# Heads' attentions: the output product's units inside the step pattern, left-over projections between the first maxima, zeros issued by GpSimd

## The chip, the cores and the metric

The kernel runs on one core of a Trainium2 chip. A core has TensorE (PE: matmuls, with weight loads, PEld, beside them), VectorE (DVE), ScalarE (ACT), GpSimd (POOL) and SyncE (SP), which only issues DMAs; ACT and POOL issue DMAs too. The engines run their own instruction streams in order and wait for each other through semaphores. The metric is the device time in microseconds of one execution, median of several runs.

## The reference

Four layers over x (4 batches of 512 tokens, 256 wide) with a context of 1601 tokens. In each, a cross-attention and a feed-forward part are added to x through tanh gates. Layers 0, 1 and 2 have attentions of 16 heads of 16; layer 3 has one of a single head. Cut to what the change touches:

```python
for l in range(3):                                # attentions of heads
    q, k, v = norm(x) @ Wq + bq, ctx @ Wk + bk, ctx @ Wv + bv   # layer 1: rope on q and k; layers 1, 2: a mask
    attn = softmax(einsum("bhqd,bhkd->bhqk", q, k) * scale, axis=-1)
    x = x + tanh(g_xattn[l]) * (concat(einsum("bhqk,bhkd->bhqd", attn, v)) @ Wo + bo)
    x = x + tanh(g_ffn[l]) * ffn_l(norm(x))       # 0: a quantised linear, 1 and 2: 8 experts
x = x + tanh(g_xattn[3]) * one_head(norm(x), ctx)
x = x + tanh(g_ffn[3]) * top2_of_8_experts(norm(x))
```

## The kernel before, in words

Each heads' attention (`head_attention`) is written once as a list of units (`Plan`), and every engine's program walks that list and emits its share of each unit. So the order of the list is the order on every engine.

**Groups and steps.** The 16 heads of a batch are 4 groups of 4 heads; a layer has 4 batches x 4 groups = 16 groups, each in `attend`. A group walks the 1601 keys in 13 steps of 128. A step has four `s2` units (PE: scores of one head, 128 keys x 512 queries, L1348; ACT: exp of them, L1441) and ends with the `pv` unit of the step before (PE: four heads' exp times values, L1362).

**First pass.** The exp needs each query's maximum, which a first pass finds for a later group: 32 `max` units per group. One is, on PE, two matmuls of 401 keys (L1326, together an M) into one of two PSUM slots `m`, and on DVE one reduction of them (L1208). Which step holds how many M is a table: `FEW` or `MANY` gives the count for each of the 13 steps, `ORDER[count]` the pattern, with S for an `s2` unit and M for a `max` unit. After a group's 32nd M, `peak` (DVE, L1219 to L1223) and `turn` (PE transpose L1332, DVE copy L1228, then three small DMAs `qaug<-tm`) bring the maxima to where the group's first S needs them.

**Output product.** When two groups' attentions are normalised, `output` yields a `norm` unit (DVE multiplies 128x512, L1235) and two `out` units. One is two matmuls on PE (L1371) into an `m` slot and an addition into x on DVE (L1242). They are one of the `work` generators of `attend`: units handed out after an S by its number n, here `OUT_AT = 3, 6, 30` (3 units, from S 6 to S 30), on top of the step's M. `output` serves groups 1 and 3. Another such generator is `normalise`: `sum` (SP: `rc<-z`, `ot<-z`), `rec` (DVE reciprocal), `low` (ACT issues `sums<-rc`), `spread` (ACT waits for that DMA and issues `ot<-sums`).

**Start of layers 1 and 2** (`lay_out_ready`). Most keys and values were projected in the layer before; those of batch 3 are left (`LEFT`, class `Prepared`, `prepare_pe` and `prepare_act`): 8 key pieces and 13 value pieces in 4 chunks of the context (512, 512, 512 and 65 tokens), each chunk one DMA `e_t<-in_ctxT`. The list: queries of batch 0 (one half split in three bf16 parts by DVE, one by GpSimd, stored in DRAM as `qready`), their fetch for all groups into `qaug`, loads, `prep` k=0 (three chunks, 18 pieces), the 32 M of group 0, `turn`, `prep` k=1 (the last chunk, 3 pieces), the output bias, then the first group.

**Zeros.** In layer 2 the `take` units of batches 1 to 3 (ACT copies a group's values, L1435) also issue, on ACT's DMA queue, one of 12 transfers of 2 MB of zeros (`clear_act`: `xregion<-zero`, `yback<-zero`), for buffers of layer 3. ACT issues them after it has waited for the batch's values.

Of the kernel before, what the change touches and what calls it, by code (L numbers as in the profile page):

```python
# [170 lines left out]
class Prepared:  # L171
# [6 lines left out]
    def __init__(self, kn, sb, w, slots, order, in_parts, rope, plan):  # L178
# [17 lines left out]
        for count, engines in plan:  # L196
            part = []
            for _ in range(count):
# [18 lines left out]
                c["end"] = s  # L217
# [15 lines left out]
def prepare_weights_sp(kn, p):  # L233
# [4 lines left out]
    prepare_load_sp(kn, p, 3)  # L238
# [70 lines left out]
def prepare_pe(kn, p, part):  # L309
# [3 lines left out]
    for c in p.parts[part]:  # L313
        f, (c0, n) = c["i"] % 4, CHUNKS[c["n_c"]]
        arrived = kn.sema(f"p_ctx{f}", DMA)
        pe.wait_ge(arrived.sem, arrived.at(c["i"] // 4 + 1))
        for x in c["keys"]:
            j, s = x["j"], x["s"]
            if s >= many:
# [5 lines left out]
        for t, s in c["values"]:  # L325
            if s >= many:
                pe.wait_ge(p_free.sem, p_free.at(s - many + 1))
# [7 lines left out]
def prepare_act(kn, p, part):  # L335
# [4 lines left out]
    for c in p.parts[part]:  # L340
        c0, n = CHUNKS[c["n_c"]]
        for x in c["keys"]:
            j, s, k = x["j"], x["s"], x["k"]
            f, slot = k % p.RING, p.slots[s % many]
# [18 lines left out]
        if c["i"] >= 2:  # L363
            act.wait_ge(kept.sem, kept.at(c["i"] // 2))
        for i, (t, s) in enumerate(c["values"]):
            act.wait_ge(p_full.sem, p_full.at(s + 1))
            act.copy(p.vb[0:KW[t], f, i, :], p.slots[s % many][0:KW[t], 0:D]).then_inc(p_free.sem, 1)
        h, t0 = KW[t], c["values"][0][0]
# [100 lines left out]
class Plan:  # L469
# [91 lines left out]
    def attend(self, g, b, peaks, counts, *work):  # L561

        given = [0] * len(work)
        for k in range(KT):
            turning, j = bool(self.to_turn), 0
            for it in ORDER[counts[k]]:
                if it == "M":
                    next(peaks, None)
                    continue
# [17 lines left out]
    def lay_out(self):  # L587
# [36 lines left out]
        for b in range(B - 1):  # L624
# [4 lines left out]
            ended = [(self.output(1, b - 1), *OUT_AT)] if b else []  # L629
            self.attend(1, b, peaks, FEW, *ended, (projected, 16, 6, JOBS - 1), (self.normalise(0, b), NORM_STEPS, 2 * HG, NORM_LAST))  # L630
            self.attend(2, b, peaks, FEW, (projected, 10, 0, 20), (self.normalise(1, b), NORM_STEPS, 2 * HG, NORM_LAST))
            self.attend(3, b, peaks, FEW, (self.chain(self.then("fetch", b=b + 1, g=2, what="kq", k=1, by="kd2"),
                                                 *(self.then("take", b=b + 1, g=g) for g in range(3))), 4, 8, 24),
                        (self.output(0, b), *OUT_AT), (self.normalise(2, b), NORM_STEPS, 2 * HG, NORM_LAST))
# [12 lines left out]
    def lay_out_ready(self):  # L647
# [17 lines left out]
        for g in range(NG):  # L665
# [3 lines left out]
        for b in range(B):  # L669
# [7 lines left out]
            for g in range(1, NG):  # L677
                renew = [self.renew(g - 1, b + 1)] if on else []
                ended = [(self.output(0 if g == 3 else 1, b if g == 3 else b - 1), *OUT_AT)] if g == 3 or g == 1 and b else []
                self.attend(g, b, peaks, FEW if on or g < NG - 1 else (0,) * KT, *ended, *renew, *((k, *given) for k in keys), (self.normalise(g - 1, b), NORM_STEPS, 2 * HG, NORM_LAST))  # L680
# [24 lines left out]
def head_attention(kn, w, gate, scale, rope, mask, ready, setup, late):  # L705
# [4 lines left out]
    with ctx:  # L710
# [51 lines left out]
        if ready:  # L762
            room = dict(p_ctx=a.e_t[:].rearrange("p a j n -> p (a j n)").rearrange("p (f c n) -> p f c n", c=DC, n=512), p_kf=a.ot)
            if rope is not None:
# [3 lines left out]
                           [a.pv[:]] + [s[:] for s in a.s_slot], LEFT, (), None, ((3, ("",)), (1, ("",))))  # L768
# [208 lines left out]
def head_ready_sp(kn, a, n_of):  # L977
# [35 lines left out]
    for u in plan.units:  # L1013
# [12 lines left out]
        elif u.kind == "prep_loads":  # L1026
            prepare_weights_sp(kn, a.p)
            prepare_sp(kn, a.p, 0)
# [93 lines left out]
def head_pool(kn, a):  # L1122
# [122 lines left out]
def head_pe(kn, a):  # L1245
# [22 lines left out]
    for u in plan.units:  # L1268
# [26 lines left out]
        elif u.kind == "prep":  # L1295

            pe.wait_ge(s_free.sem, s_free.at(u.s))
            prepare_pe(kn, a.p, u.k)
            p_free = kn.sema("p_free")
            if u.k == 1:  # L1300
                pe.wait_ge(p_free.sem, p_free.at(a.p.n))
# [11 lines left out]
        elif u.kind == "max":  # L1313
            if (u.b, u.g) not in started:
# [5 lines left out]
                by, n = a.arrived[u.b, u.g, "k"]  # L1320
                pe.wait_ge(kn.sema(by, DMA).sem, kn.sema(by, DMA).at(n))
# [53 lines left out]
def head_act(kn, a):  # L1375
# [10 lines left out]
    for u in plan.units:  # L1386
# [28 lines left out]
        elif u.kind == "prep":  # L1415
            prepare_act(kn, a.p, u.k)
# [6 lines left out]
        elif u.kind == "take":  # L1423
# [6 lines left out]
            if a.clears and u.b:  # L1430
                clear_act(kn, a, (u.b - 1) * NG + u.g)
# [40 lines left out]
def clear_act(kn, a, nth):  # L1472

    act, cleared = kn.nc.scalar, kn.sema("cleared", DMA)
    parts = GATED_ROWS // REGION
    to, lo = (kn.dram["xregion"], REGION * nth) if nth < parts else (kn.dram["yback"], REGION * (nth - parts))
    if nth < CLEARED:
        width = to.shape[1]
        act.dma_start(to[lo:lo + REGION, :].rearrange("(p r) c -> p r c", p=P),
# [1660 lines left out]
```

## Time and profile before

| | us |
|---|---|
| median of 3 runs | 3765.19 (3760.28 to 3768.38) |
| the profiled execution | 3765.78 |
| its span in the profile | 3764.6 |
| PE busy | 3387.0 (90% of the span) |
| DVE busy | 2168.7 (58%) |
| ACT busy | 2024.8 (54%) |
| POOL busy | 943.5 (25%) |

The heads' attentions lie at 0 to 826 us (layer 0), 1006 to 1750 us (layer 1) and 2062 to 2806 us (layer 2) of the span. A number at a row's start is microseconds since the span's start; busy time says how long an engine had work, not that it was what the others waited for.

### The profile page before, as it was taken

How to read it: one execution, taken by the hardware profiler on the slowest of the kernel's cores; microseconds unless marked ns; L12 is line 12 of the kernel's file. 1: busy time of each engine (PE TensorE's matmuls, PEld its weight loads, DVE VectorE, ACT ScalarE, POOL GpSimd, SP SyncE). 2: the span in 40 equal slices, each digit the busy share in tenths (PEclk: the TensorE clock that was granted, in tenths of full speed). 3: DMA queues.
4: the chain of work that ended last, by engine and by line, in shares of the span. 5: the costliest groups of instructions: out<-in, count | busy, mean ns of one | idle time of the engine just before them, and what ended most of it. 6: DMA issues, size and time to landing. Idle time of an engine off the chain costs nothing.

```text
span 3764.6 us, 52382 instructions
## 1 busy us (share of the span) xinstructions
PE 3387.0 (90%) x18396; PEld 1786.1 (47%) x18396; DVE 2168.7 (58%) x3463; ACT 2024.8 (54%) x4490; POOL 943.5 (25%) x1061
## 2 busy tenths in 40 slices
PE   5999999978699999997898799999978979897997
PEld 2333333325432333333697323333327956697996
DVE  6667676837767787883302577878842033364333
ACT  2577767753236677775333266767752322254664
POOL 2232322004638462001302262410002010022332
PEclk8899999989789999998899799999998989998998
DMA  8142323115655453203764665654118421132555
GB/s 197 41 107 66 104 74 96 26 59 165 175 170 130 102 121 76 52 17 117 229 234 134 188 167 136 157 126 109 48 40 296 155 93 53 33 116 103 183 183 170
DMA packets 265310, 456.02 MB, mean 121 GB/s; under 512 B 54027, under 2 KB 174643, under 8 KB 262875
## 3 DMA queue, kind: packets, MB, share of 16 engines
q1 hardware_dynamic: 163878, 224.05, 22.3%
q0 software_dynamic: 49520, 166.30, 13.4%
q10 hardware_dynamic: 51653, 62.32, 5.8%
q8 instruction: 150, 2.46, 0.3%
q14 instruction: 109, 0.89, 0.1%
HBM read 292.46 MB, written 153.91 MB: 119 GB/s over the span
## 4 chain that ended last, share of the span: by engine, by line
PE 76%; DVE 8%; DMA 6%; ACT 3%; POOL 3%; issue 2%; SPq 1%; ACTq 0%; POOLq 0%; DVEq 0%
PE pv L1362 15%; PE s L1348 14%; PE m L1326 13%; PE h L2849 5%; PE y L2857 5%; PE h L2423 4%; PE y L2432 4%; DVE mxp L1208 3%; PE y L1829 3%; PE s L1809 2%; PE s L1293 2%; PE m L1371 2%; DMA sums<-rc 1%; PE s L1310 1%; ACT e_t L1441 1%
## 5 line engine op out<-in xcount | busy, mean ns | idle before, releaser
L1208 DVE TENSOR_REDUCE mxp<-m 128x1 f32<-128x802 f32 x1536 | 1445.1, 987 | 487.4 <-PE m L1326 485.2
L1441 ACT ACTIVATE e_t<-s 128x512 f32<-128x512 f32 (+1 forms) x2496 | 1330.0, 600 | 514.7 <-PE s L1348 492.0
L1348 PE MATMUL s<-qaug,kaug 100*128 100x512 bf16 (+1 forms) x2496 | 834.6, 386 | 34.5 <-ACT e_t L1441 28.0
L1326 PE MATMUL m<-kaug,qaug 97*128 97x401 bf16 x3072 | 811.2, 347 | 34.6 <-DVE mxp L1208 16.8
L1362 PE MATMUL pv<-e_t,v 128*32 128x512 f32 (+1 forms) x4992 | 671.6, 610 | 0.2
L1326 PEld LDWEIGHTS m<-kaug,qaug 97*128 97x128 bf16 x3072 | 258.9, 99 | 551.2 <-DVE mxp L1208 303.7
L1348 PEld LDWEIGHTS s<-qaug,kaug 100*128 100x128 bf16 (+1 forms) x2496 | 244.6, 100 | 579.3 <-ACT e_t L1441 390.3
L127 POOL TENSOR_TENSOR rstd<-rstd,mhalf 128x16 f32<-128x16 f32 (+2 forms) x9 | 24.3, 2697 | 1105.5 <-DVE rstd L120 1105.5
L2919 ACT ACTIVATE ez<-h,b 128x128 f32<-128x128 f32 x440 | 120.1, 388 | 160.4 <-PE h L2849 160.4
L1362 PEld LDWEIGHTS pv<-e_t,v 128*32 128x32 f32 (+1 forms) x4992 | 98.7, 108 | 215.1 <-ACT e_t L1441 156.2
L2310 DVE SCALAR_TENSOR_TENSOR y<-y,b 128x256 f32<-128x256 f32 x39 | 16.6, 425 | 302.3 <-PE y L2432 302.3
L2721 DVE TENSOR_SCALAR ez<-ez 128x1024 f32<-128x1024 f32 x55 | 38.2, 694 | 225.6 <-ACT z L2919 225.6
L1085 POOL TENSOR_TENSOR kr<-kf,ks 128x512 f32<-128x512 f32 (+1 forms) x78 | 78.8, 1011 | 343.0 <-ACT ks L1413 339.1
L2506 ACT ACTIVATE hT<-h,b 128x128 f32<-128x128 f32 x312 | 84.9, 383 | 128.3 <-PE h L2423 128.2
L2423 PE MATMUL h<-xtT,w 128*128 128x128 f32 x1248 | 149.2, 279 | 0.4 <-ACT xtT L2523 0.3
L2857 PE MATMUL y<-w,hT 128*128 x624 | 143.0, 383 | 5.8 <-DVE hT L2722 5.8
L2849 PE MATMUL h<-xtT,w 128*128 128x128 f32 x1248 | 147.8, 277 | 0.0
L2423 PEld LDWEIGHTS h<-xtT,w 128*128 128x128 f32 x1248 | 146.0, 196 | 1.1 <-ACT xtT L2523 1.0
L2849 PEld LDWEIGHTS h<-xtT,w 128*128 128x128 f32 x1248 | 144.7, 194 | 0.1
L2432 PE MATMUL y<-w,hT 128*128 x624 | 140.9, 379 | 0.0
L2857 PEld LDWEIGHTS y<-w,hT 128*128 128x128 f32 x624 | 116.7, 192 | 21.0 <-issue 6.4
L2919 ACT ACTIVATE z<-h,b 128x128 f32<-128x128 f32 x440 | 122.8, 453 | 0.0
(384 smaller groups left out, 3834.0 us busy)
## 6 DMA issues: line engine op xcount, KB each, us to landing
w<-in_L_w POOLq DMA_DIRECT2D x78, 1024.0 KB, 5.3
w<-in_L_w SPq DMA_DIRECT2D x24, 1024.0 KB, 12.5
xregion<-zero ACTq DMA_DIRECT2D x10, 2056.0 KB, 12.4
kaug<-kparts SPq DMA_DIRECT2D x16, 1200.8 KB
kaug<-kready SPq DMA_DIRECT2D x32, 600.4 KB
kaug<-kready SPq DMA_DIRECT2D x16, 1200.8 KB
vn<-values SPq DMA_DIRECT2D x8, 1536.0 KB
values<-p_vb ACTq DMA_DIRECT2D x21, 512.0 KB, 5.3
```

The costliest lines, as they stand in the source:

```text
L1208: dve.tensor_reduce(a.mxp[:, u.g % 2, half, n:n + 1], a.m_slot[u.m % 2][:].rearrange("p (a n) -> p a n", a=2)[:, :, 0:PIECE + 1], AX.XY, A ...
L1326: m = pe.matmul(slot[:, 512 * k:512 * k + PIECE + 1], a.qaug[0:R_MAX, u.g, j, P * qc:P * qc + P], a.kaug[0:R_MAX, u.g, j, k0:k0 + PIECE + ...
L1348: pe.matmul(slot[0:KW[u.k], :], a.kaug[0:R_ALL, u.g, u.j, P * u.k:P * u.k + KW[u.k]], a.qaug[0:R_ALL, u.g, u.j, :], start=True, stop=True) ...
L1362: m = pe.matmul(a.pv[32 * j:32 * j + 32, :], a.v[0:KW[u.k], u.k, u.g, VW * j:VW * j + 32], a.e_t[0:KW[u.k], u.n % 2, j, :], start=u.k == 0 ...
L1441: act.activation(a.e_t[0:KW[u.k], e % 2, u.j, :], a.s_slot[u.s % 3][0:KW[u.k], :], ACT.Exp).then_inc(s_free.sem, 1)
L1829: m = pe.matmul(a.y_slot[:, 0:D], a.eT[0:KW[i], k % 2, i, :], a.v[0:KW[i], b % 2, i, :], start=i == 0, stop=i == KT - 1)
L2423: m = pe.matmul(a.h_slot[i % 2][:, P * f:P * f + P], a.w1[:, w1_at, c, P * f:P * f + P], xT(c), start=c == 0, stop=c == DC - 1)
L2432: m = pe.matmul(a.y_slot[i % 2][:, 0:D], a.hT[:, i % 2, f, :], w2(f), start=f == 0, stop=f == FC - 1)
L2506: t = act.activation(a.hT[:, p, f, :], slot[:, P * f:P * f + P], func, bias=bias(f))
L2849: m = pe.matmul(a.h_slot[i % 2][:, P * f:P * f + P], w1[:, c, P * f:P * f + P], xT(c), start=c == 0, stop=c == DC - 1)
L2857: m = pe.matmul(a.y_slot[i % 2][:, 0:D], a.hT[:, i % 2, f, :], w2(f), start=f == 0, stop=f == FC - 1)
L2919: t = act.activation(to[:, p, P * f:P * f + P], slot[:, P * f:P * f + P], func, bias=bias(f))
```

## The change

Four edits.

1. **Output units in the pattern.** In groups with an output product, `output` is no longer a `work` generator. Steps 3 and 6 use `OUT_ORDER = "MSSOSSM"`: the pattern for three M with O, one `out` unit, in place of the middle M. The counts of such groups are `FEW_OUT`, also 32 M. `norm` now has no place of its own: it stands right before the first `out`. Five groups of layer 0 and six each of layers 1 and 2 are changed, 17 in all; the last batch of layer 0 and the last group of layers 1 and 2 keep the old way.
2. **First maxima.** The first group of a layer has five M in its first step, two of them ahead of the first S (`"MMSMSSMS"`), where there were four.
3. **Left-over projections between the first maxima** (layers 1 and 2). Six pieces stand ahead, the other 15 one after every second M. Both halves of the first queries are split by DVE; group 0's queries are stored and fetched first; only one context chunk is loaded ahead of that, the other three behind it.
4. **Zeros on GpSimd.** The 12 transfers are issued by GpSimd, in its order of units, without the wait for the values.

```diff
-MANY = (4, 4, 3, 4, 3, 4, 3, 4, 3, 1, 1, 2, 2)
-ORDER = ("SSSS", "SMSSS", "SMSMSS", "MSSMSSM", "MSMSMSSM")
+MANY = (5, 4, 3, 4, 3, 4, 3, 4, 3, 1, 1, 2, 2)
+ORDER = ("SSSS", "SMSSS", "SMSMSS", "MSSMSSM", "MSMSMSSM", "MMSMSSMS")
...
+OUT_STEPS = (3, 6)
+OUT_ORDER = "MSSOSSM"
+FEW_OUT = (3, 3, 3, 2, 3, 3, 2, 3, 2, 2, 1, 2, 3)
+LEFT_PIECES = KT + DC * len(CHUNKS)
+LEFT_AHEAD = 6
...
     def output(self, c, b):
         self.add("norm", b=b, g=2 * c + 1)
-        yield
         for k in range(TT // 2):
...
-            for it in ORDER[counts[k]]:
+            for it in ORDER[counts[k]] if out is None or k not in OUT_STEPS else OUT_ORDER:
...
+                if it == "O":
+                    next(out)
+                    continue
...
         for c in range(DC):
-            self.split("q", 0, c, 0, ("dve", "pool"))
-        self.add("fetch", b=0, g=0, what="q", k=NG, by="qd")
+            self.split("q", 0, c, 0, ("dve",))
+            if c == 0:
+                self.add("fetch", b=0, g=0, what="q", k=1, by="qd")
+                self.add("prep_more")
+            else:
+                self.add("fetch", b=0, g=1, what="q", k=NG - 1, by="qd")
+        self.add("fetch", b=0, g=1, what="k", k=1, by="kd1")
         self.add("loads", b=0)
-        for g in range(1, NG):
+        for g in range(2, NG):
             self.add("fetch", b=0, g=g, what="k", k=1, by=f"kd{g}")
-        self.add("prep", k=0)
-        for _ in self.maxima(0, 0):
-            pass
+        pieces = iter(range(LEFT_PIECES))
+        for _ in range(LEFT_AHEAD):
+            self.add("prep", k=next(pieces))
+        for n, _ in enumerate(self.maxima(0, 0)):
+            if n % 2:
+                k = next(pieces, None)
+                if k is not None:
+                    self.add("prep", k=k)
         self.turn()
-        self.add("prep", k=1)
+        for k in pieces:
+            self.add("prep", k=k)
         self.add("bias")
+        self.add("prep_end")
...
+        elif u.kind == "take" and a.clears and u.b:
+            pool.wait_ge(filled.sem, filled.at(2))
+            clear_pool(kn, a, (u.b - 1) * NG + u.g)
...
-            if a.clears and u.b:
-                clear_act(kn, a, (u.b - 1) * NG + u.g)
```

**PE at the start of layer 1.** L322 and L330 (L327 and L337 after) are a left-over key and value piece, L1326 (L1376) an M. Before:

```order
L330 MATMUL s_107<-p_wv,e_t 128x256 x2
L322 MATMUL s_108<-e_t,p_wk 128x512 x2
L322 MATMUL s_109<-e_t,p_wk 128x512 x2
L330 MATMUL pv<-p_wv,e_t 128x256 x2
L330 MATMUL s_107<-p_wv,e_t 128x256 x2
L330 MATMUL s_108<-p_wv,e_t 128x256 x2
```

After, from the same piece on:

```order
L337 MATMUL s_107<-p_wv,e_t 128x256 x2
L1376 MATMUL m_110<-kaug,qaug 128x401 x2
L1376 MATMUL m_111<-kaug,qaug 128x401 x2
L327 MATMUL s_108<-e_t,p_wk 128x512 x2
L1376 MATMUL m_110<-kaug,qaug 128x401 x2
L1376 MATMUL m_111<-kaug,qaug 128x401 x2
L327 MATMUL s_109<-e_t,p_wk 128x512 x2
```

The first M stood behind 18 pieces and now stands behind 6; the others lie between pairs of M.

**SP at the same place**, with its waits: L252 loads a context chunk, L94 stores queries, L1050 (L1088) fetches them. Before:

```order
L252 DMA e_t_99<-in_ctxT 128x2x512 x3
L252 DMA e_t_99<-in_ctxT 128x2x65
L94 DMA qready<-ks_94 128x3x512 [waits split_dve]
L94 DMA qready<-ks_94 128x2x512
L94 DMA qready<-ks_94 128x512
L1050 DMA qaug_96<-qready 96x16x512 [waits pooled1,stored0]
```

After:

```order
L252 DMA e_t_99<-in_ctxT 128x2x512
L94 DMA qready<-ks_94 128x3x512 [waits split_dve]
L94 DMA qready<-ks_94 128x2x512
L94 DMA qready<-ks_94 128x512
L1088 DMA qaug_96<-qready 96x4x512 [waits stored0]
L252 DMA e_t_99<-in_ctxT 128x2x512 x2
L252 DMA e_t_99<-in_ctxT 128x2x65
```

The fetch of group 0's queries no longer waits for GpSimd's half, and three chunks moved behind it.

**DVE around the first output unit of a group** (layer 1). L1208 (L1255) reduces an M, L1235 (L1282) is `norm`, L1242 (L1289) the output unit's addition. Before:

```order
L1235 TENSOR_TENSOR ot<-ot 128x512 [waits summed,moved]
L1208 TENSOR_REDUCE mxp<-m_110 128x1 [waits m_full]
L1208 TENSOR_REDUCE mxp<-m_111 128x1 [waits m_full]
L1208 TENSOR_REDUCE mxp<-m_110 128x1 [waits m_full]
L1208 TENSOR_REDUCE mxp<-m_111 128x1 [waits m_full]
L1208 TENSOR_REDUCE mxp<-m_110 128x1 [waits m_full]
L1242 SCALAR_TENSOR_TENSOR x<-m_111,gates,x 128x512 [waits m_full]
```

After:

```order
L1255 TENSOR_REDUCE mxp<-m_111 128x1 [waits m_full]
L1255 TENSOR_REDUCE mxp<-m_110 128x1 [waits m_full]
L1282 TENSOR_TENSOR ot<-ot 128x512 [waits summed,moved]
L1289 SCALAR_TENSOR_TENSOR x<-m_111,gates,x 128x512 [waits m_full]
L1278 RECIPROCAL rc<-rc 128x16 [waits summed]
```

`norm` moved from five reductions ahead of the addition to right before it, behind the reduction of the step's first M.

## Rows read from the trace of the kernel before

**Rows 1.** The page, part 4: the chain that ended last, by engine.

```profile
PE 76%; DVE 8%; DMA 6%; ACT 3%; POOL 3%; issue 2%; SPq 1%; ACTq 0%; POOLq 0%; DVEq 0%
```

**Rows 2.** Timeline, layer 1's start: start us, us, engine line op, [idle before <-releaser].

```profile
1036.95 3.60 PE L322 MATMUL s<-e_t,p_wk 128*128 128x512 f32 x8
...
1050.73 0.85 PE L1326 MATMUL m<-kaug,qaug 97*128 97x401 bf16 x4
...
1051.27 30.71 DVE L1208 TENSOR_REDUCE mxp<-m 128x1 f32<-128x802 f32 x32 [23.54 <-PE m L1326]
...
1090.18 0.63 PE L1348 MATMUL s<-qaug,kaug 100*128 100x512 bf16 x1
```

**Rows 3.** Timeline, layer 2's start.

```profile
2091.43 3.60 PE L322 MATMUL s<-e_t,p_wk 128*128 128x512 f32 x8
...
2105.20 0.85 PE L1326 MATMUL m<-kaug,qaug 97*128 97x401 bf16 x4
...
2144.65 0.63 PE L1348 MATMUL s<-qaug,kaug 100*128 100x512 bf16 x1
```

**Rows 4.** Timeline, layer 0's start, value pieces between its M.

```profile
76.34 26.00 DVE L1208 TENSOR_REDUCE mxp<-m 128x1 f32<-128x802 f32 x28 [0.72 <-PE m L1326]
...
106.47 0.88 PE L1326 MATMUL m<-kaug,qaug 97*128 97x401 bf16 x2
108.14 0.61 PE L1348 MATMUL s<-qaug,kaug 100*128 100x512 bf16 x1 [0.80 <-DMA qaug<-tm]
```

**Rows 5.** Timeline, SP's issues at layer 1's start.

```profile
1027.76 1.69 SPq L94 DMA_DIRECT2D qready<-ks  x3
1039.05 0.33 SPq L1050 DMA_DIRECT2D qaug<-qready  x1
```

**Rows 6.** Windows, layer 1's start: stretch, us, busy by engine, PEclk, DMA share, GB/s.

```profile
1065.00:1070.00 5.00, 4.34 (x12) 0.65 (x10) 4.91 (x6) 0.00 (x0) 0.00 (x0) 0.50 1.03 209
1075.00:1080.00 5.00, 4.35 (x11) 0.65 (x10) 4.90 (x6) 0.00 (x0) 0.00 (x0) 0.50 0.00 1
```

**Rows 7.** Timeline, layer 1, batch 2, group 3: step 3 and the next.

```profile
1563.08 1.06 PE L1362 MATMUL pv<-e_t,v 128*32 128x512 f32 x8
...
1564.31 0.51 PE L1326 MATMUL m<-kaug,qaug 97*128 97x401 bf16 x2
...
1564.85 1.89 DVE L1208 TENSOR_REDUCE mxp<-m 128x1 f32<-128x802 f32 x2 [0.51 <-PE m L1326]
...
1565.90 1.13 PE L1371 MATMUL m<-wo,ot 128*128 128x256 f32 x4 [0.31 <-DVE mxp L1208]
1566.87 0.38 PE L1348 MATMUL s<-qaug,kaug 100*128 100x512 bf16 x1
...
1567.18 1.07 PE L1362 MATMUL pv<-e_t,v 128*32 128x512 f32 x8
...
1570.27 1.06 PE L1362 MATMUL pv<-e_t,v 128*32 128x512 f32 x8
```

**Rows 8.** DVE groups by form, 1400 to 1750 us: count, busy us, mean ns.

```profile
L1235 DVE TENSOR_TENSOR ot<-ot 128x512 f32<-128x512 f32 x4 | 2.7, 682 | 0.0
```

**Rows 9.** Windows, whole groups: layer 2 (first three), layer 1 (last three).

```profile
2196.34:2241.07 44.73, 40.47 (x223) 12.53 (x222) 31.57 (x40) 28.83 (x56) 28.05 (x39) 0.92 0.73 182
2318.98:2368.42 49.44, 43.41 (x230) 13.94 (x229) 31.64 (x40) 29.98 (x58) 39.95 (x45) 0.93 0.72 200
2487.34:2537.86 50.52, 43.91 (x231) 14.12 (x230) 31.64 (x40) 30.03 (x58) 15.03 (x16) 0.90 0.53 143
1147.52:1190.10 42.58, 39.45 (x222) 12.20 (x222) 32.02 (x40) 28.80 (x56) 39.42 (x44) 0.96 0.67 158
1482.08:1522.47 40.39, 39.78 (x231) 13.54 (x230) 33.14 (x43) 28.88 (x56) 0.00 (x0) 1.00 0.25 49
1522.47:1560.00 37.53, 37.53 (x223) 12.22 (x222) 31.07 (x40) 28.66 (x56) 0.00 (x0) 1.00 0.28 53
```

**Rows 10.** Chain of waits, layer 2: start us, us, what.

```profile
2333.40 18.65 DMA sums<-rc
```

More of the change, by code:

```diff
@@ L216, in __init__ @@
                     s += 1
-                c["end"] = s
+                c["end"], c["many"] = s, len(c["keys"]) + len(c["values"])
                 self.chunks.append(c)
@@ L306, in prepare_held_sp, with prepare_pe @@
         prepare_store_sp(kn, p, x)
-def prepare_pe(kn, p, part):
+def prepare_pe(kn, p, part, only=None):
     pe, p_full, p_free, p_w = kn.nc.tensor, kn.sema("p_full"), kn.sema("p_free"), kn.sema("p_w", DMA)
@@ L313, in prepare_pe @@
     for c in p.parts[part]:
+        if only is not None and not c["end"] - c["many"] <= only < c["end"]:
+            continue
         f, (c0, n) = c["i"] % 4, CHUNKS[c["n_c"]]
@@ L318, in prepare_pe @@
             j, s = x["j"], x["s"]
+            if only not in (None, s):
+                continue
             if s >= many:
@@ L325, in prepare_pe @@
         for t, s in c["values"]:
+            if only not in (None, s):
+                continue
             if s >= many:
@@ L332, in prepare_pe, with prepare_act @@
             m.then_inc(p_full.sem, 1)
-def prepare_act(kn, p, part):
+def prepare_act(kn, p, part, only=None):
     act, p_full, p_free, p_w = kn.nc.scalar, kn.sema("p_full"), kn.sema("p_free"), kn.sema("p_w", DMA)
@@ L341, in prepare_act @@
         c0, n = CHUNKS[c["n_c"]]
+        if only is not None and not c["end"] - c["many"] <= only < c["end"]:
+            continue
         for x in c["keys"]:
             j, s, k = x["j"], x["s"], x["k"]
+            if only not in (None, s):
+                continue
             f, slot = k % p.RING, p.slots[s % many]
@@ L362, in prepare_act @@
         kept = kn.sema(f"p_v{f}", DMA)
-        if c["i"] >= 2:
+        if c["i"] >= 2 and only in (None, c["values"][0][1]):
             act.wait_ge(kept.sem, kept.at(c["i"] // 2))
         for i, (t, s) in enumerate(c["values"]):
+            if only not in (None, s):
+                continue
             act.wait_ge(p_full.sem, p_full.at(s + 1))
             act.copy(p.vb[0:KW[t], f, i, :], p.slots[s % many][0:KW[t], 0:D]).then_inc(p_free.sem, 1)
+        if only not in (None, s):
+            continue
         h, t0 = KW[t], c["values"][0][0]
@@ L559, in output, with attend @@
             yield
-    def attend(self, g, b, peaks, counts, *work):
+    def attend(self, g, b, peaks, counts, *work, out=None):
         given = [0] * len(work)
@@ L679, in lay_out_ready @@
                 ended = [(self.output(0 if g == 3 else 1, b if g == 3 else b - 1), *OUT_AT)] if g == 3 or g == 1 and b else []
-                self.attend(g, b, peaks, FEW if on or g < NG - 1 else (0,) * KT, *ended, *renew, *((k, *given) for k in keys), (self.normalise(g - 1, b), NORM_STEPS, 2 * HG, NORM_LAST))
+                last_one = not on and g == NG - 1
+                self.attend(g, b, peaks, (0,) * KT if last_one else FEW_OUT if ended else FEW, *(ended if last_one else []), *renew, *((k, *given) for k in keys), (self.normalise(g - 1, b), NORM_STEPS, 2 * HG, NORM_LAST),
+                            out=ended[0][0] if ended and not last_one else None)
             last = (self.renew(NG - 1, b + 1), (self.normalise(NG - 1, b), NORM_STEPS, 2 * HG, NORM_LAST))
@@ L1026, in head_ready_sp @@
         elif u.kind == "prep_loads":
-            prepare_weights_sp(kn, a.p)
-            prepare_sp(kn, a.p, 0)
+            prepare_weights_sp(kn, a.p, 1)
+        elif u.kind == "prep_more":
+            prepare_load_sp(kn, a.p, len(a.p.chunks))
         elif u.kind == "loads":
@@ L1143, in head_pool @@
         elif u.kind in ("q", "k") and u.by == "pool":
+            i = splits.index(u)
+            for x in splits[i + 1:][0:1] if a.ready else ():
+                if x.kind == "k" and splits[i - 1].by == "dve":
+                    by_dve = kn.sema("split_dve")
+                    pool.wait_ge(by_dve.sem, by_dve.at(splits[i - 1].n + 1))
+                    head_load_pool(kn, a, x)
             head_split(kn, a, u, pool, "pool")
@@ L1319, in head_pe @@
                     pe.wait_ge(kn.sema(by, DMA).sem, kn.sema(by, DMA).at(n))
-                by, n = a.arrived[u.b, u.g, "k"]
-                pe.wait_ge(kn.sema(by, DMA).sem, kn.sema(by, DMA).at(n))
+                for it in ("q", "k"):
+                    if (u.b, u.g, it) in a.arrived:
+                        by, n = a.arrived[u.b, u.g, it]
+                        pe.wait_ge(kn.sema(by, DMA).sem, kn.sema(by, DMA).at(n))
             j, qc, half = u.k // (2 * QC), u.k // 2 % QC, u.k % 2
@@ L1415, in head_act @@
         elif u.kind == "prep":
[L1416 removed]
+            prepare_act(kn, a.p, 0, u.k)
         elif u.kind == "v":
```

30 lines of the change are left out of this document (16 added, 14 removed).

## The prediction

> **What bounds the kernel now.** I read the page's chain first: PE carries 76% of it [rows 1], so the kernel is as long as PE's program plus the time in which PE waits or runs slowly. Then windows over whole groups of the attentions show two kinds. In an undisturbed group of layer 1 PE is busy for the whole 37.53 us at full clock, or 39.78 of 40.39 us where output units are in it; in three groups of layer 2 it idles 4.3, 6.0 and 6.6 us at a mean clock of 0.90 to 0.93 [rows 9]. In the steady part only PE's own instructions and their order count. The rest lies in the disturbed groups, and at the starts of layers 1 and 2, which the timeline shows: PE first works off pieces of left-over projections, then feeds the 32 first M, and there DVE is the bound, with 32 reductions back to back in 30.71 us while PE is fed at half clock [rows 2, 6].
>
> **Left-over projections between the M.** Before, PE comes to its seventh piece at 1036.95 and to the first M at 1050.73; after, the M follow the sixth piece. That is 13.78 us earlier, if queries and keys are there. In layer 2 it is 2105.20 - 2091.43 = 13.77 us [rows 2, 3].
> The M then take longer only where a piece makes PE slower than DVE. Layer 0 has this very pattern, with value pieces, and its 28 reductions took 26.00 us, 0.93 each [rows 4], a little less than the 0.96 before (30.71 / 32). A key piece takes 1.8 us of PE (3.60 for two [rows 2]), to which two M of some 0.35 us come (802 columns each at full clock, 2.4 GHz, are 0.33): 2.5 us per pair against 1.86 on DVE. Four large key pieces lie there, so 4 x 0.65 = 2.6 us. From first M to last reduction: 32 x 0.93 + 0.5 + 2.6 = 32.9 us, against 1051.27 + 30.71 - 1050.73 = 31.25. That costs 1.6 us.
> Behind the last reduction, layer 1 needed 1090.18 - 1081.98 = 8.20 us to its first S, with three pieces in the way. In layer 0, with none, it was 108.14 - 102.34 = 5.80 us [rows 4]. That gives 2.4 us. Sum per layer: 13.8 - 1.6 + 2.4 = 14.6 us. What can be late next are DMAs. The fetch of the first queries was issued at 1039.05, after GpSimd's half had been stored; now it waits for DVE's first half alone, whose store was issued at 1027.76 [rows 5] and will be earlier, so it can land before 1037. The three context chunks now follow it. The DMA engines were full until shortly before 1075 (share 1.03, then 0.00 [rows 6]) and the small transfers of the maxima, which now come near 1071, stand in SP's queue behind that load. I take off 0.6 us in each layer: 14 us, two layers, **28 us less**. The bounds are 2 x 7 (queries or chunks 7 us late) and 2 x 16.
>
> **One more early M.** While PE waits for the maxima to be moved (0.80 us at 108.14), it now has a second M. At the half clock of that place an M takes 0.88 us [rows 4]. Three layers, 0 to 2.6 us; I take **2 us less**.
>
> **Output units.** Step 3 took 1567.18 - 1563.08 = 4.10 us, and a step with three M takes 1570.27 - 1567.18 = 3.09 us [rows 7]. Over whole groups an output unit cost (40.39 - 37.53) / 2 = 1.43 us [rows 9], though PE is held by it for only 1566.87 - 1565.90 = 0.97. It stood as a third user of two slots, 0.31 us of it waiting for a reduction. In the place of the middle M it needs no slot that isn't free: 3.09 - 0.35 + 0.97 = 3.7 us, 0.4 less than 4.10. The counts with three, two and one M are the same in both tables, so nothing else changes.
> But the first unit of a group now has `norm` right ahead of it in DVE's order, and PE waits for it. After the step's first M starts, DVE takes 0.54 us to begin its reduction (1564.31 to 1564.85), 0.95 for it (1.89 for two) and 0.68 for `norm` [rows 7, 8]; PE follows 0.1 us later, as at 1565.90. That is 2.27 us, where PE would come to the unit after one M and two S, 0.35 + 2 x 0.22 = 0.79 us (an S is 512 columns, 0.21). So PE, with everything behind it, stands 1.5 us: 3.7 + 1.5 = 5.2 us instead of 4.1. Before, `norm` lay five reductions earlier and nothing waited for it. Per group +1.1 - 0.4 = +0.7 us, in 17 groups **12 us more**. Below, without any stall: 17 x (-0.8) = -14. Above, with DVE one reduction (0.95) further behind: +28. I take the middle, since each of its pieces has a row.
>
> **Zeros on GpSimd.** In layer 2 `sums<-rc`, 8 KB, landed 18.65 us after issue, and so in the chain [rows 10]; in ACT's program the batch's zeros, 2 MB, are issued shortly ahead of it on the same queue. ACT waits for it in `spread`, ahead of exps that PE needs. The three disturbed groups lost 44.73 - 37.53 = 7.2 us, and, allowing 3.6 us for two query projections at 1.8, 49.44 - 41.1 = 8.3 and 50.52 - 41.1 = 9.4: 25 us in all [rows 9]. The like group of layer 1, with no zeros at all, lost 42.58 - 37.53 = 5.05 us, so that much of the first remains. That leaves 20 us. Not all of it comes back: GpSimd waits for nothing of ACT, so it sends the zeros of a batch in a row as soon as its splits are done, and five of them (10 MB) right behind its last split, near 2500 us, when the batch's values are loaded too. I take **15 us less**; bounds 0 and 25. What stays hidden: 12 issues gone from ACT, which has idle time in each step, and come to GpSimd, behind whose last ones nothing waits for 300 us.
> Here a page speaks against the change. The Trainium skill (DMA: Bandwidth & Descriptors, Issuing engines are not separate DMA queues) says that all DMAs run on the same 16 engines whoever issues them, and that another issuer saves only the sequencer's time. Another section of it (Queues, rings and completion order) says that a DMA engine goes round its queues packet by packet, by which a small transfer passes a large one of another queue. No row of before decides between them; the first is a rival below.
>
> **Sum.** Against the profiled execution's own 3765.8 us (span 3764.6, and 1.2 around it; the median is 0.6 lower): -28 - 2 + 12 - 15 = -33, so 3733 us.
>
> **Rivals.**
> *The zeros only change their issuer.* Same DMA engines, same bytes, so `sums<-rc` lands as late and only the issue time on ACT is saved, which ACT has to spare. For it: the DMA share was 0.53 to 0.73 over those groups, and the group without zeros still lost 5 us. Against: in that group it was at 0.67, and it lost less than the two later ones. Time: 3733 + 15 = 3748. By the page's first rule this is what happens.
> *The output units run without a stall,* if DVE is ahead when the step begins, or `norm` overlaps the S. For it: DVE is busy only 31.07 of 37.53 us. Against: the reduction of the step's own M is in front of `norm`, and starts 0.54 us after it whatever DVE's slack. Time: 3733 - 17 x 1.5 = 3708 with all of it, 3714 if a part stays.
> *The DMA engines become the bound at the starts.* The load up to 1075 is the same, and the maxima's small transfers cannot pass it in SP's queue. If it also slips by the gap in which SP waits for the first store (up to 7 us), half of the gain goes: 3733 + 14 = 3747.
> *Slower: the run of zeros is served in order of arrival.* Place: layer 2, batch 2 to 3, five transfers of 2 MB in a row. At the 143 to 200 GB/s of those stretches [rows 9] each takes 10 us or more; a small transfer behind all five is 50 us late, of which the steps between `low` and `spread` hide about 10. PE then stands 40 us: 3748 + 40 = 3788. It decides from two queued ahead on. Against: no row of before shows a transfer of one queue held up for the whole of another queue's.
> *The change doesn't do what it says:* the order shows pieces, units and issues moved as described, so this is left with no chance.
>
> **Numbers.** Chances: forecast 0.50, zeros without gain 0.17, no stall 0.13, bound by DMA at the starts 0.12, slower 0.05, and 0.03 for gains that cancel to nothing. Range: 3714 to 3752 holds the first four and what lies between. 0.2% is 7.5 us and about what a measurement of this kernel can tell from no change. Faster by more: 0.90; within: 0.05; slower: 0.05.
>
> **What would show it.** In layers 1 and 2 the first M starts 14 us earlier against the first piece, reductions run at 0.93 us with four gaps near 0.6, and the first S comes 5.8 us behind the last. In step 3 of the 17 groups the `out` matmul waits about 1.5 us for the `norm` line of DVE, in step 6 for nothing; groups take 41.1 us, not 40.4. In layer 2 `sums<-rc` lands in under 10 us and the three groups come to some 43, 42 and 44 us. I am wrong if the first M waits for a DMA, if step 3 shows no wait, or if the three groups keep their length.

## The result, and the profile after

The changed kernel takes 3774.7 us (median of 8 runs, 3769.8 to 3778.1), the kernel before 3767.5 beside it; the ratio is 1.0019, with a 95% interval of 1.0010 to 1.0028. So it is 0.2% slower, where 3733 us were forecast. The profiled execution has a span of 3773.7 us against 3764.6.

The page's chain by engine, after (answers to [rows 1]), and its line of the chain by instruction:

```profile
PE 74%; DMA 8%; DVE 8%; ACT 3%; issue 2%; POOL 2%; SPq 2%; ACTq 0%; POOLq 0%; DVEq 0%
PE pv L1412 15%; PE s L1398 14%; PE m L1376 13%; PE h L2897 5%; PE y L2905 5%; PE h L2471 4%; PE y L2480 4%; DVE mxp L1255 3%; PE y L1877 2%; PE s L1857 2%; PE s L1340 2%; DMA rc<-z 2%; PE m L1421 1%; DMA qaug<-tm 1%; PE s L1358 1%
```

PE's share fell by two points and that of the DMAs rose by two. The names are new too: before, the one DMA that the chain's line named was `sums<-rc`; now it names `rc<-z` and `qaug<-tm`, transfers of 8 KB and 4 KB.

To find where that is, I followed the start of each group's first `pv` from layer to layer. From the first `pv` of a layer to its last, layer 0 takes 700.6 us (before: 700.0), layer 1 644.0 (644.5), layer 2 684.9 (645.6). The first `pv` of layer 1 comes 14.6 us earlier than before, that of layer 2 28.4. So everything up to 2123 us is a gain, about as forecast, and layer 2's attentions give back 39 us. These are readings of one execution each, and they scatter: in e2 and e7 below, whose programs are that of the kernel before up to layer 2, the first `pv` of layer 1 comes at 1088.7 and 1088.9 us instead of 1096.9. The windows over whole groups show it (columns as in [rows 9], to which they answer: the first, third and fifth are the three groups of layer 2 shown there, the second, fourth and sixth the groups behind them, the last two are in layer 1):

```profile
2167.18:2212.39 45.21, 40.57 (x222) 12.38 (x221) 32.21 (x41) 29.24 (x56) 32.93 (x44) 0.94 0.92 214
2212.39:2262.09 49.70, 43.12 (x224) 13.11 (x223) 31.20 (x40) 29.04 (x55) 0.00 (x0) 0.85 0.39 103
2302.33:2354.99 52.66, 45.69 (x232) 14.69 (x232) 32.80 (x41) 31.18 (x59) 39.43 (x44) 0.89 0.72 204
2354.99:2409.80 54.81, 44.00 (x229) 14.23 (x228) 33.99 (x42) 28.58 (x54) 30.40 (x41) 0.84 0.89 200
2488.86:2538.79 49.93, 45.67 (x232) 14.68 (x232) 32.66 (x41) 31.18 (x59) 20.79 (x21) 0.89 0.81 197
2538.79:2588.64 49.85, 43.16 (x228) 14.27 (x228) 32.60 (x41) 28.18 (x54) 0.00 (x0) 0.91 0.49 157
1466.75:1506.99 40.24, 38.90 (x228) 13.47 (x227) 32.59 (x42) 28.62 (x55) 0.00 (x0) 1.00 0.23 46
1506.99:1544.95 37.96, 37.96 (x225) 12.38 (x224) 31.74 (x41) 29.04 (x56) 0.00 (x0) 1.00 0.30 55
```

The three groups with long waits were 44.73, 49.44 and 50.52 us before: two are longer now, and the third is 0.6 us shorter. The three behind them, nearly undisturbed before, are now 10 to 15 us longer than their like of layer 1. In the groups in which PE has these long waits its mean granted clock is lower as well, 0.84 in the longest, so such a stall costs more than its own length.

The chain of layer 2 names the DMAs on it (start us, us, what; the pieces of PE and DVE between them left out):

```profile
2166.26 9.46 DMA rc<-z
...
2179.34 11.74 DMA sums<-rc
...
2198.56 6.83 DMA qaug<-tm
...
2209.98 17.03 DMA rc<-z
...
2334.06 12.03 DMA qaug<-tm
...
2387.99 13.58 DMA qaug<-tm
...
2520.45 9.44 DMA qaug<-tm
...
2535.71 18.61 DMA rc<-z
```

And the timeline shows what was issued just ahead of one of them (rows of GpSimd, SyncE and PE, about 2332 us):

```profile
2332.27 1.17 POOL L1527 DMA_DIRECT2D xregion<-zero  x1
...
2332.86 2.70 SPq L1115 DMA_DIRECT2D qaug<-tm  x3
...
2346.14 1.03 PE L1398 MATMUL s<-qaug,kaug 100*128 100x512 bf16 x2 [6.78 <-DMA qaug<-tm]
```

GpSimd issues 2 MB of zeros 0.6 us before SyncE issues the 4 KB of `qaug<-tm`. Such a transfer lands in 1.7 us (median) in layer 1, where there are no zeros; the last of these three took 12.0, and PE stands 6.8 us in front of its S.

What the small transfers do behind the run of five near 2510 us is of weight for the causes below. These are the DMA issues of two windows, 2509.4 to 2515 us and 2519.1 to 2521.1 us (size of one, median us from issue to landing):

```profile
xregion<-zero POOLq DMA_DIRECT2D x3, 2056.0 KB, 24.5
yback<-zero POOLq DMA_DIRECT2D x2, 2048.0 KB, 42.8
...
qaug<-tm SPq DMA_DIRECT2D x3, 4.0 KB, 9.1
```

The three of 4 KB were issued after all five of 2 MB and had landed by 2529.9 us. Of the five only the first had landed then; the others followed between 2535 and 2559 us. So the small ones were held up by some 7 us, but did not wait for all that was queued ahead of them.

Layer 1's start, after (answers to [rows 2]):

```profile
1025.62 3.75 PE L327 MATMUL pv<-e_t,p_wk 128*128 128x512 f32 x4 [8.02 <-DMA e_t<-in_ctxT]
...
1034.41 0.85 PE L1376 MATMUL m<-kaug,qaug 97*128 97x401 bf16 x4
...
1066.72 1.89 DVE L1255 TENSOR_REDUCE mxp<-m 128x1 f32<-128x802 f32 x2 [1.38 <-PE m L1376]
...
1075.83 0.61 PE L1398 MATMUL s<-qaug,kaug 100*128 100x512 bf16 x1 [1.53 <-DMA qaug<-tm]
```

Step 3 of the group in layer 1, batch 2, group 3, after (answers to [rows 7]):

```profile
1549.59 0.99 DVE L1255 TENSOR_REDUCE mxp<-m 128x1 f32<-128x802 f32 x1 [0.29 <-PE m L1376]
1550.50 0.68 DVE L1282 TENSOR_TENSOR ot<-ot 128x512 f32<-128x512 f32 x1
1551.33 1.10 PE L1421 MATMUL m<-wo,ot 128*128 128x256 f32 x4 [1.34 <-DVE ot L1282]
...
1553.13 1.06 PE L1412 MATMUL pv<-e_t,v 128*32 128x512 f32 x8
```

The output unit waits 1.34 us for `norm`, which stands behind the reduction of the step's own M, as forecast.

### The profile page after: what moved, and what is told of

The parts are those of the page before. It is cut to its first block, busy times and chain, and to the rows that moved or that the text cites. A ratio compares the mean times of both kernels' runs of the same rounds, so it can differ in the third digit from the quotient of the medians.

```text
span 3773.7 us, 52460 instructions
## 1 busy us (share of the span) xinstructions
PE 3363.4 (89%) x18396; PEld 1791.2 (47%) x18396; DVE 2176.6 (58%) x3476; ACT 2028.8 (54%) x4490; POOL 938.3 (25%) x1054
## 4 chain that ended last, share of the span: by engine, by line
PE 74%; DMA 8%; DVE 8%; ACT 3%; issue 2%; POOL 2%; SPq 2%; ACTq 0%; POOLq 0%; DVEq 0%
PE pv L1412 15%; PE s L1398 14%; PE m L1376 13%; PE h L2897 5%; PE y L2905 5%; PE h L2471 4%; PE y L2480 4%; DVE mxp L1255 3%; PE y L1877 2%; PE s L1857 2%; PE s L1340 2%; DMA rc<-z 2%; PE m L1421 1%; DMA qaug<-tm 1%; PE s L1358 1%
## 5 line engine op out<-in xcount | busy, mean ns | idle before, releaser
L1255 DVE TENSOR_REDUCE mxp<-m 128x1 f32<-128x802 f32 x1536 | 1448.7, 987 | 470.9 <-PE m L1376 468.8
L1376 PE MATMUL m<-kaug,qaug 97*128 97x401 bf16 x3072 | 801.2, 344 | 42.2 <-DVE mxp L1255 24.1
L1376 PEld LDWEIGHTS m<-kaug,qaug 97*128 97x128 bf16 x3072 | 259.6, 99 | 576.2 <-DVE mxp L1255 308.4
L2905 PEld LDWEIGHTS y<-w,hT 128*128 128x128 f32 x624 | 117.1, 193 | 20.7 <-issue 6.5
L2480 PEld LDWEIGHTS y<-w,hT 128*128 128x128 f32 x624 | 116.1, 191 | 14.0
## 6 DMA issues: line engine op xcount, KB each, us to landing
xregion<-zero POOLq DMA_DIRECT2D x10, 2056.0 KB, 15.5
```

The source lines that it names most:

```text
L1255: dve.tensor_reduce(a.mxp[:, u.g % 2, half, n:n + 1], a.m_slot[u.m % 2][:].rearrange("p (a n) -> p a n", a=2)[:, :, 0:PIECE + 1], AX.XY, A ...
L1376: m = pe.matmul(slot[:, 512 * k:512 * k + PIECE + 1], a.qaug[0:R_MAX, u.g, j, P * qc:P * qc + P], a.kaug[0:R_MAX, u.g, j, k0:k0 + PIECE + ...
L2480: m = pe.matmul(a.y_slot[i % 2][:, 0:D], a.hT[:, i % 2, f, :], w2(f), start=f == 0, stop=f == FC - 1)
L2905: m = pe.matmul(a.y_slot[i % 2][:, 0:D], a.hT[:, i % 2, f, :], w2(f), start=f == 0, stop=f == FC - 1)
```

## The experiments

**What theories there were.** From the two profiles: A, the zeros' transfers cost what layer 2 lost, because GpSimd issues them at moments at which a small transfer of the maxima or sums comes next, and that one lands late. B, something else of the change (start, units, early M) disturbs layer 2. Within A: A1, only the moment counts; A2, transfers that GpSimd issues are worse wherever they stand.

**e1 (the label's first part names each run): the zeros back on ScalarE, at `take`; all else as changed.**

```diff
-        elif u.kind == "take" and a.clears and u.b:
-            pool.wait_ge(filled.sem, filled.at(2))
-            clear_pool(kn, a, (u.b - 1) * NG + u.g)
...
+            if a.clears and u.b:
+                clear_act(kn, a, (u.b - 1) * NG + u.g)
```

> The changed kernel, but the 12 transfers of zeros are issued by ACT at the `take` units, as in the kernel before. Layer 2's attentions took 684.9 us from first to last pv in the changed kernel and 645.6 in the one before, so if the zeros' new issuer and moment are the whole loss (theory A), the time falls by 39 us, to 3736 us (3730 to 3742), and the two starts keep their 28 us. Rival B, that the output units or the earlier start of layer 2 brought the loss: the time stays above 3760 us.

Measured: 3741.0 us (3737.7 to 3744.1), ratio to before 0.9941 (0.9924 to 0.9957). Layer 2's attentions take 649.7 us, not 684.9. That is A, for 35 of the 39 us; the other edits disturb layer 2 by at most 4 us (645.6 before). The three longest DMAs of its chain are the kind that the kernel before had, `sums<-rc`:

```profile
2178.67 14.36 DMA sums<-rc
...
2304.48 19.32 DMA sums<-rc
...
2477.63 17.42 DMA sums<-rc
```

**e2: the kernel before, with this one edit of the change (zeros issued by GpSimd).**

> The kernel before, with only the zeros moved to GpSimd. Theory A: layer 2's attentions get some 39 us longer, 3800 to 3808 us. Rival B: within 8 us of the kernel before, since then the loss needs the other edits.

Measured: 3792.1 us (3790.0 to 3797.4), ratio 1.0081 (1.0064 to 1.0098): 28.7 us slower than before, in layer 2 (673.3 us against 645.6). The edit costs time by itself. The size is less than the 37 us or more that I had expected. That the zeros fall at another place against the groups in each kernel is my explanation; it was not tested.

**e3: the changed kernel, GpSimd's zeros held back to a fixed step of the group.** In front of each transfer GpSimd waits for the batch's values and for the fourth `pv` behind the group whose values are replaced, so that it falls beside `sums<-rc`.

```diff
             pool.wait_ge(filled.sem, filled.at(2))
+            pool.wait_ge(vl.sem, vl.at(2 * u.b + 2))
+            pool.wait_ge(pv_done.sem, pv_done.at(read.n + 5))
             clear_pool(kn, a, (u.b - 1) * NG + u.g)
```

> The changed kernel, but GpSimd waits before each transfer of zeros until the batch's values are there and the next group's fourth pv is done, so that each is issued within some 2 us of where ACT issued it (after the reciprocal, well ahead of the maxima's small transfers). Theory A1, it is the moment: zeros in flight hold every small transfer, and GpSimd issued them right ahead of those of the maxima (12 us instead of 1.7) and of `rc<-z`; then this run has neither these nor the `sums<-rc` behind zeros on ACT's queue: 3718 to 3732 us. Rival A2, it is the software queue that crowds out the others: the loss stays, 3760 us or more.

Measured: 3722.1 us (3720.0 to 3724.7), ratio 0.9891 (0.9874 to 0.9907). The same issuer, the same bytes, and some 50 us less than the changed kernel. That rules out A2 and shows A1. Ten of the twelve transfers are issued within 0.5 us of `sums<-rc`. Of the other two one came 6.2 us behind it and one 15.5, and just at the latter the chain has its longest DMA:

```profile
2312.02 1.17 POOL L1532 DMA_DIRECT2D xregion<-zero  x1
...
2312.60 2.69 SPq L1115 DMA_DIRECT2D qaug<-tm  x3
...
2325.79 1.03 PE L1403 MATMUL s<-qaug,kaug 100*128 100x512 bf16 x2 [6.69 <-DMA qaug<-tm]
```

**e4: the zeros on ScalarE, but right behind `sums<-rc` instead of ahead of it.**

```diff
             head_low_act(kn, a, u)
+            if a.clears:
+                clear_act(kn, a, u.n)
```

> The changed kernel, with the zeros on ACT's queue, but right behind `sums<-rc` (the `low` unit) instead of at `take`, in the first 12 groups. By A1 the zeros are done before the next maxima's transfers and nothing needed stands behind them on ACT's queue but `ot<-sums`: 3715 to 3728 us, 8 to 20 less than e1. By A2 the same. A third theory, A3, that any 2 MB anywhere in a group costs a stall of 5 us or so in the groups with other traffic: 3735 us or more.

Measured: 3714.2 us (3711.3 to 3717.7), ratio 0.9867 (0.9850 to 0.9883), 1 us below the forecast's range and 27 less than e1; A3 is out. Layer 2's attentions take 625.7 us, 20 less than before the change and 24 less than e1's. The timeline about 2300 us shows the place that the zeros have now: the next small transfer comes 15.7 us behind them, and by the page's row one transfer of zeros lands after 12.3 us (median).

```profile
2300.09 0.33 ACTq L1508 DMA_DIRECT2D sums<-rc  x1
...
2300.45 0.70 ACTq L1526 DMA_DIRECT2D xregion<-zero  x1
...
2316.15 1.79 SPq L1115 DMA_DIRECT2D qaug<-tm  x3
```

The page of e4, part 6, and below it the issues of 2300.4 to 2302 us and of 2316 to 2318.2 us: size of one and median us to its landing.

```profile
xregion<-zero ACTq DMA_DIRECT2D x10, 2056.0 KB, 12.3
...
xregion<-zero ACTq DMA_DIRECT2D x1, 2056.0 KB, 23.7
...
qaug<-tm SPq DMA_DIRECT2D x3, 4.0 KB, 7.0
```

Just at this place, where the next batch's values are loaded too (`vn<-values`, issued 1 to 2 us ahead), the gap is not enough: the zeros need 23.7 us, `qaug<-tm` takes 7.0, and PE stands 2.8 us. In the other groups the gap holds.

**e7: the kernel before, with the zeros at that place and nothing else changed.** Its edit is that of e4.

> The kernel before with one edit: ScalarE issues the 2 MB of zeros right behind `sums<-rc` of each head instead of at `take`. Theory M (the moment alone decides): the stalls of the layer-2 groups that the zeros cause go, as they do with the other edits in place; 3763 - 24 = 3739 us (3735 to 3746), where 24 is -49 for all edits with the zeros there, less -28 for the starts, -2 for the early M and +5 for the units. Rival I (it needs the earlier start, which moves the zeros away from other loads): within 8 us of 3763.

Measured: 3739.7 us (3729.3 to 3745.4), ratio 0.9939 (0.9922 to 0.9956). In layer 2's attentions the moment is worth 24 us without the rest of the change (645.6 to 622.0) and with it (649.7 to 625.7, e1 to e4); rival I is out. The three disturbed groups of [rows 9] take 37.6, 42.7 and 41.1 us here: that is about what they are when the zeros stand in nobody's way.

**e9: the changed kernel, each transfer of zeros cut into four.** What it asks is whether a small transfer waits for the one big transfer in hand or for all the bytes ahead of it.

```diff
-        pool.dma_start(to[lo:lo + REGION, :].rearrange("(p r) c -> p r c", p=P),
+        for r0, r1 in zip(cuts, cuts[1:]):
+            pool.dma_start(to[lo:lo + REGION, :].rearrange("(p r) c -> p r c", p=P)[:, r0:r1, :],
```

> The changed kernel with each 2 MB transfer of zeros by GpSimd split into four of a quarter of the rows, issued one behind the other at the same place. What is asked is how a 4 KB transfer on SyncE's queue comes to take 9 to 14 us behind one of 2 MB on GpSimd's. Theory Q (it is served behind all bytes already queued, whichever way they are cut): `qaug<-tm` of layer 2's groups still lands in 9 to 14 us, and the time stays within 8 us of 3775. Theory D (it waits only for the one transfer in hand): it lands in under 5 us, most of the 35 to 39 us of layer 2 comes back, 3738 to 3750 us. The 36 extra issues cost GpSimd about 1.2 us each, spread over 300 us, with nothing waiting behind them for long.

Measured: 3777.7 us (3768.0 to 3783.2), ratio 1.0018 (1.0008 to 1.0028): as slow as uncut. The chain has the same long landings (start us, us, what). So theory D is out, and to cut the transfers in four does not help. The numbers that theory Q gave came in, but its mechanism, that a small transfer is served behind all bytes already queued, does not hold either: in the run of 20 quarters (issued 2514.5 to 2529.4 us) `qaug<-tm` came behind 14 of them and landed in 9.5 us (median; 10.4 in the chain), while only 6 of the 14 had landed by then. What sets the 9 to 12 us stays open.

```profile
2213.75 22.03 DMA rc<-z
...
2341.38 11.59 DMA qaug<-tm
...
2402.29 18.70 DMA rc<-z
```

**e10: the kernel before, with the part on the starts alone.** Units, early M and zeros are as before.

> The kernel before with one part of the change alone: the pieces of the left-over projections between the M of the starts, with the early fetch of the first queries; units, early M and zeros as before. The forecast's term: 28 us less (14 in each of layers 1 and 2), 3763 - 28 = 3735 us (3731 to 3739), the first step of layer 1's attentions 14 to 15 us earlier, that of layer 2 28. Rival: the earlier start runs into the zeros and loads of layer 2 and gives a part back there: 3742 to 3752 us.

Measured: 3742.4 us (3738.7 to 3745.3), beside 3768.8 for the kernel before; ratio 0.9933 (0.9920 to 0.9946), 26 us less; 28 were forecast. The time itself lies at the lower end of the rival's 3742 to 3752, because the kernel before took 6 us more beside it than the 3763 from which both theories started; by the ratio it would be 3738, inside the forecast's range. In the trace the first `pv` of layer 2 comes 29.4 us earlier, and layer 2's attentions take 650.1 us against 645.6, nearly all of it in one group (53.8 us against 49.4, with a `sums<-rc` of 20.1 us where it was 18.7): the rival's effect is there, at 4 us in one execution.

**e6: e4, with the output units put back to their old place.**

> The kernel with the zeros issued by ScalarE right behind `sums<-rc` (3714 us), with the output units put back where they were in the kernel before: third users of the two slots, beside all M of their step, `norm` five reductions ahead. Theory by the traces (the pair of groups 78.2 against 77.9 us): the new place costs 0.28 us a group, so this is 17 x 0.28 = 5 us faster, 3709 us. Theory of the forecast (0.7 us a group): 12 us faster, 3702 us. Rival: the new place is a gain outside layer 1's even groups: slower than 3714.

Measured: 3712.7 us (3701.6 to 3715.6), ratio 0.9858 (0.9838 to 0.9878), against 0.9867 for e4: 3 us less by the ratios, which their intervals tell neither from nothing nor from 12. The traces decide for the 5 us: layers 0 and 1 are 2.3 and 2.5 us shorter than in e4, layer 2 as long. In the pair of groups the new place costs 40.24 + 37.96 = 78.20 us against 40.39 + 37.53 = 77.92 [rows 9].

**e5: e4, with `norm` five reductions ahead of its output unit again, the units in their new place.**

```diff
         self.add("norm", b=b, g=2 * c + 1)
+        yield
...
+                if out is not None and n == 6:
+                    next(out)
```

> The kernel with the zeros issued by ScalarE right behind `sums<-rc` (3714 us), and `norm` moved from right ahead of its output unit in step 3 to S number 6 of the group, five reductions earlier, as it was in the kernel before; the units keep their place in the pattern. Theory N: step 3 takes 5.1 us because the unit waits for `norm`, which stands behind the reduction of the step's own M; with `norm` done before, the step falls to 3.6 us like step 6, in 17 groups: 17 x 1.5 = 25 us less, 3689 us (3684 to 3698). Rival: the unit waits for its slot or for the next reduction, whatever `norm` does; step 3 keeps over 4.5 us and the time stays within 6 us of 3714.

Measured: 3690.5 us (3687.7 to 3701.0), ratio 0.9812 (0.9795 to 0.9830), at the forecast of theory N. In the trace the unit no longer waits, the step is 3.5 us instead of 5.1, and the group 38.84 us, all of it PE's. The timeline of that step, and the window of its group (columns as in [rows 9]):

```profile
1537.42 1.06 PE L1412 MATMUL pv<-e_t,v 128*32 128x512 f32 x8
...
1539.21 1.03 PE L1421 MATMUL m<-wo,ot 128*128 128x256 f32 x4
...
1540.94 1.06 PE L1412 MATMUL pv<-e_t,v 128*32 128x512 f32 x8
```

```profile
1534.15:1572.99 38.84, 38.84 (x228) 13.40 (x227) 32.49 (x42) 28.65 (x55) 0.00 (x0) 1.00 0.24 47
```

This kernel is the fastest of all here, 1.9% below the kernel before and 2.1% below the changed one by the ratios.

**e8: e4, without the early M.**

> The kernel with the zeros issued by ScalarE right behind `sums<-rc` (3714 us), with four M instead of five in the first step of each layer's first group. Forecast's theory: the fifth M fills a wait of PE, so it is worth 2 us and this takes 3716 us (3714 to 3718). Rival from the traces (layer 0's first step 4.7 us with it, 3.1 without): the fifth M only lengthens the step, and this takes 3710 to 3713 us.

Measured: 3720.8 us (3718.3 to 3723.2), ratio 0.9887 (0.9870 to 0.9904) against 0.9867. So the rival (the M only lengthens the step) finds no support: all runs of e8 lie above all of e4. The ratios are 7 us apart, but each has an interval of 0.0017 either way, so that the forecast's 2 us are as possible. The fifth M stands ahead of the first `pv`, so the place to look is the stretch from the last of the first 32 reductions to that `pv`: 13.2 us against 12.3 in layer 0, 11.5 against 12.3 in layer 2, and in layer 1 it scatters from 13.0 to 17.8 us among kernels with the same edits there. From the first `pv` on, the traces show 1 us either way (layer 0: 701.8 us against 700.7; layer 2: 624.6 against 625.7). So its size, and by the traces even its sign, stays open.

## Why the prediction was wrong

**The step that failed is the zeros: "I take 15 us less; bounds 0 and 25".** By e1 against the changed kernel it is 29 us more by the ratios (1.0019 - 0.9941), and 35 in layer 2's steps. This term's error, some 44 us, is more than that of the whole (42); the other terms were off by 7 us the other way (units) and 2 this way (starts).

The wait that I priced did go. In the kernel before, two steps of 9.7 and 10.6 us (in the groups from 2318.98 and 2487.34) waited for `sums<-rc`; after, both are 3.1 us, and ScalarE comes to its next issue behind `sums<-rc` 9.0 us after it (2316.76 to 2325.73), where it was 18.7. What I had at nothing are the new waits, and they cost more than the old ones.

Three things in that step were wrong.
- *I looked for the one small transfer that the zeros had delayed and not for those that they could delay.* A group has three in its critical order: `qaug<-tm` for the maxima, some 10 us later `rc<-z`, 12 to 15 us after that `sums<-rc`, and 16 us on the next `qaug<-tm` (e4's timeline). ScalarE issued the zeros 3 us ahead of `sums<-rc`, for which ScalarE waits only in `spread`, with about 9 us of cover (cover: the time from a transfer's issue until someone needs it). Moved to GpSimd, they met `qaug<-tm`, in front of which PE has 5 us of cover (in the chain from 2334.1, waited for from 2346.1 - 6.8 = 2339.4), and `rc<-z`, which took 17.0 and 18.6 us. There DVE stands, 7.2 us in the first case (2219.8 to 2227.0), with the reductions behind it.
- *I priced the order of GpSimd's program but not the clock time at which it issues.* GpSimd waits for nothing of ScalarE, as the prediction says; that was read as harmless. It means that nothing keeps the zeros away from the small transfers (e3 adds just such a wait, and the loss is gone). They came at 2176.4, 2197.9, 2202.9, 2332.3, 2361.6, 2383.0, 2388.1 and from 2509.5 five in a row. Of the seven single ones five stand within 8 us ahead of a long landing in the chain, and the five in a row 11 us ahead of one and 26 ahead of another.
- *Both bounds were about the old wait alone: 25 if all of it goes, 0 if nothing does.* A new wait had no bound. "No row of before shows a transfer of one queue held up for the whole of another queue's" was an argument from a trace in which no such pair stood close together, and it was about the wrong thing: the `qaug<-tm` of 2334.06 landed 1.7 us before the zeros issued ahead of it did, and a delay of 10 us is enough where the cover is 5. The slower rival (3788, chance 0.05) was right in its sign. That its price of 40 us for layer 2 is what was lost (39) is luck: at the run of five, where it had a small transfer 50 us late and PE standing 40 us, `qaug<-tm` landed in 9.1 us and PE stood 4.2. Instead there were five steps that are 6 to 11 us too long, with shorter ones beside them, and a single transfer ahead was enough where I had put the deciding point at two.

The signs by which I had said the term could be told speak against it too: the three groups were to come to some 43, 42 and 44 us and came to 45.2, 52.7 and 49.9.

The Trainium skill (DMA: Bandwidth & Descriptors, Issuing engines are not separate DMA queues) says that the engines are shared whoever issues. e3 and e4 agree with that: 3722 and 3714 us from two issuers at nearly the same moment. Its other section (Queues, rings and completion order) has an engine go round its queues packet by packet. The rows of the run of five agree in kind: the 4 KB on SyncE's queue landed in 9.1 us, ahead of four of the five transfers of 2 MB queued before them. They are also what I had missed: to pass is not to be undisturbed, 9 to 12 us instead of 1.7.

**The starts: right, 28 forecast, 26 measured (e10).** In layer 1, from the first piece to the first M it is 8.8 us instead of 22.2, 13.4 less (forecast 13.8). From first M to the end of the last reduction it is 1068.6 - 1034.4 = 34.2 us (forecast 32.9), with gaps of 0.5 to 0.8 in the early part and one of 1.38. The first S comes 7.2 us behind, not 5.8, 1.5 of it waiting for `qaug<-tm`. In layer 2 these two are 32.7 and 5.5 us, as forecast. From the first piece to the first `pv` layer 1 gains 68.4 - 56.7 = 11.7 us and layer 2 68.7 - 54.5 = 14.2, together 26. That layer 1's first piece also starts 2.9 us earlier in this trace is no gain: it starts at 1020.3 to 1028.6 us in the traces of kernels whose program is the same up to there.

**The output units: mechanism right, size too large.** Step 3 was forecast at 5.2 us and takes 5.1, with the stall where it was said; step 6 was 3.7 and takes 3.5. But the other eleven steps of the group are together 0.6 us shorter, and the last step of the group before it is 0.4 longer, so that a pair of groups loses 0.28 us, not 0.7: 5 us over 17 groups, not 12. The group itself takes 40.24 us, where 41.1 were forecast. The clause "so nothing else changes" was too simple: of the other eleven steps one fewer has three M (3.09 us) and one more has two (2.66), and in the last step of the group before it is the other way round. That the stall is `norm`'s and is worth what it was priced at is shown by e5: 17 x 1.5 = 25 us forecast, 21 to 24 measured.

**The early M:** 2 us forecast; a gain by e8's times, its size open.

**The sum again with what was measured:** -26 (starts) + 5 (units) - 2 (early M, as forecast) + 29 (zeros) = +6 us, and the kernels differ by 7. That is closer than the parts are known: each ratio has an interval of some 3 to 8 us either way.

## What to carry to other kernels

When a large transfer changes its issuer, its price is the moment: list every small transfer that someone waits for, with its issue time and its cover, and put the large one right behind the last of them, where the gap to the next is longer than its landing (with every other load that lands there counted in). An engine that runs ahead of the others is the wrong place for it unless a wait ties it to the step. And an order edit that puts a producer right ahead of its consumer makes the consumer wait for what stands ahead of the producer on its engine (1.34 us here); leave the producer where it was, and move only the consumer.

## What the hardware showed

- A small transfer issued on another queue shortly after a large one is held up, but not for all that is queued: `qaug<-tm`, 4 KB, lands in 1.7 us alone, in 12.0 with one transfer of 2 MB issued 1.8 us ahead, in 13.6 with one 5 us ahead and another beside it, and in 9.1 behind five (10 MB), of which four landed after it. `rc<-z`, 8 KB, took 9.5 us behind a load of keys of 1.2 MB without zeros (the chain's 2166.26) and 15.9 to 22.0 behind zeros and keys (e9 included). It made no difference whether the 2 MB was one transfer or four.
- On the same queue it is otherwise: in the kernel before, ScalarE issued `sums<-rc` 3.1 to 3.4 us behind the zeros, and in the three long waits (14.7, 18.7 and 17.1 us) what waited for it went on 0.2 to 1.0 us after the zeros had landed.
- A long wait of PE costs more than it lasts: in the group from 2354.99 us PE is busy 44.0 us for work that takes 38.9 us in layer 1, at a mean granted clock of 0.84 instead of 1.00.
